# Weight products placed between the halves of the neighbour products, y high copied ahead of relu, and neighbour marks turned by DMA transposes

## The reference

```
d2  = sq[:, :, None] + sq[:, None, :] - 2.0 * einsum('bdn,bdm->bnm', xyz, xyz)   # xyz: 1601 x 512 per batch
_, idx = top_k(-d2, 8)
for i in range(4):                       # done twice, with the same weights
    p = lrelu(points, 0.01)
    g = the eight neighbours' columns of p
    points = (w_center[i] @ p + (w_neighbor[i] @ g).sum(over neighbours)) / 9 + points
```

## Time and profile before

| | |
|---|---|
| median of 3 runs | 337.64 us (336.52 to 339.07) |
| profiled execution, its own time | 334.24 us |
| its span, first to last instruction | 332.5 us |
| around the span | 1.74 us |
| TensorE matmul busy | 320.8 us (97%) |
| VectorE / ScalarE / GpSimd busy | 258.5 / 174.0 / 95.0 us |
| Gram phase, to the first step's first matmul | 107.17 us |
| granted TensorE clock | 1.00 throughout |

### The profile page before, as it was taken

The page is one execution under the profiler, slowest core; times in us unless marked ns, Lnnn a source line. Parts: engine busy times, 40 slices in busy tenths (PEclk is TensorE's granted clock), DMA queues, the critical chain, the costliest instruction groups (busy, mean ns, idle before and its releaser), DMA issues.

```text
span 332.5 us, 5114 instructions
## 1 busy us (share of the span) xinstructions
PE 320.8 (97%) x2024; PEld 290.9 (88%) x2024; DVE 258.5 (78%) x333; ACT 174.0 (52%) x255; POOL 95.0 (29%) x85
## 2 busy tenths in 40 slices
PE   4999999999999899999899999999999999999995
PEld 4999999999899788888788889888888888889884
DVE  3994799799699676888867796887869867796773
ACT  4584397485564726454836644626455264644510
POOL 2011111111133214333644441426335063441400
PEclk9999999999999999999999999999999999999999
DMA  7979859969700000000000000000000000000023
GB/s 236 353 209 264 223 146 239 279 150 251 188 0 1 2 0 2 0 0 2 1 2 0 1 3 0 0 2 0 2 0 0 2 0 2 0 0 2 38 92 126
DMA packets 8608, 23.41 MB, mean 70 GB/s; under 512 B 772, under 2 KB 2052, under 8 KB 8584
## 3 DMA queue, kind: packets, MB, share of 16 engines
q1 hardware_dynamic: 7288, 18.36, 16.3%
q0 software_dynamic: 1296, 4.72, 8.3%
HBM read 20.98 MB, written 2.10 MB: 69 GB/s over the span
## 4 chain that ended last, share of the span: by engine, by line
PE 41%; DVE 8%; ACT 2%; issue 1%; DVEq 0%
PE wide L423 24%; PE wide L412 6%; PE wide L401 5%; PE wide L399 5%; DVE y_rest L722 2%; DVE y_lo L726 2%; DVE r_mixed L662 2%; DVE state L734 2%; ACT y_hi L570 2%; ACT relu L562 1%; PE wide L385 0%; ACT r_high L565 0%; DVEq L709 0%; DVEq L725 0%
## 5 line engine op out<-in xcount | busy, mean ns | idle before, releaser
L279 POOL TENSOR_TENSOR r_low<-relu,r_high 128x512 fp32r<-128x512 f32 x64 | 84.8, 1339 | 140.4 <-ACT r_high L565 140.4
L423 PE MATMUL wide<-adj,y_hi 128*128 128x512 f32 (+1 forms) x260 | 102.3, 394 | 0.8 <-DVE state L734 0.8
L423 PE MATMUL wide<-adj,y_lo 128*128 128x512 f32 (+1 forms) x260 | 101.7, 393 | 0.0
L722 DVE TENSOR_TENSOR y_rest<-wide,y_hi 128x1024 f32<-128x1024 f32 x32 | 39.2, 1224 | 45.4 <-ACT y_hi L570 45.4
L562 ACT ACTIVATE relu<-state 128x512 f32<-128x512 f32 x64 | 40.2, 628 | 46.5 <-DVE state L734 33.7
L399 PE MATMUL wide<-w_high,r_high 128*128 128x256 f32 x256 | 62.2, 281 | 0.9 <-DVE y_rest L722 0.9
L401 PE MATMUL wide<-w_low,r_low 128*128 128x256 f32 x256 | 61.9, 280 | 0.0
L570 ACT CAST y_hi<-wide 128x1024 fp32r<-128x1024 f32 x32 | 32.3, 1008 | 54.8 <-PE wide L401 54.8
L423 PEld LDWEIGHTS wide<-adj,y_hi 128*128 128x128 f32 x260 | 48.9, 188 | 11.7 <-DVE state L734 1.2
L423 PEld LDWEIGHTS wide<-adj,y_lo 128*128 128x128 f32 x260 | 49.0, 188 | 10.5 <-issue 0.2
L399 PEld LDWEIGHTS wide<-w_high,r_high 128*128 128x128 f32 x256 | 48.3, 189 | 2.3 <-issue 1.1
(11 more groups left out here) (57 smaller groups left out, 290.6 us busy)
## 6 DMA issues: line engine op xcount, KB each, us to landing
raw<-in_ctx_dram SPq DMA_DIRECT2D x23, 512.0 KB, 5.4
g_low<-in_ctx_dram POOLq DMA_DIRECT2D x9, 512.0 KB, 6.2
state<-in_x_dram SPq DMA_DIRECT2D x4, 512.0 KB, 7.1
out_dram<-state SPq DMA_DIRECT2D x3, 512.0 KB, 2.8
w_raw<-in_fside_BxSxS_dram SPq DMA_DIRECT2D x1, 1024.0 KB, 11.2
rest_raw<-in_ctx_dram SPq DMA_DIRECT2D x4, 130.0 KB
raw<-in_ctx_dram SPq DMA_DIRECT2D x2, 256.0 KB, 3.3
out_dram<-state SPq DMA_DIRECT2D x1, 256.0 KB, 2.0
```

What stands on the lines that cost most here:

```text
L279: nc.gpsimd.tensor_tensor(r_low[:, n % 3, h, :], relu[:, h, :], r_high[:, n % 3, h, :].bitcast(fp32), ALU.subtract).then_inc(r_low_ready, 1)
L423: mm = nc.tensor.matmul(bank[to][:, cols], part[:, s % 2, q, h * P:(h + 1) * P], adj[:, b, q, cols], start=(q == 0 and part is y_hi), stop ...
L722: nc.vector.tensor_tensor(y_rest[:, :, :], wide[MAIN][:, :].rearrange("p (q o) -> p q o", q=NB), y_hi[:, s % 2, :, :].bitcast(fp32), ALU.s ...
```

## The change

1. **TensorE order in a step.** `y_step` is cut into `y_main` and `y_mixed`. A step is now: main products of s, first half of the neighbour products of s-1, mixed products of s, second half of the neighbour products of s-1.
2. **ScalarE order in a step.** `y_high(s)` comes first, then `relu_parts(s + 1)`.
3. **VectorE order in a step.** y_rest, update of half 0, y_lo, update of half 1, `relu_mixed(s + 1)`. For batch 3, distances and neighbours come one step earlier.
4. **Turning the marks.** The TensorE transposes are gone. SyncE issues four DMA transposes per batch, SBUF to SBUF, of 128x512 bf16 each (128 KB), into a new tile `turned`. For batch 0 they stand in SyncE's queue ahead of the point loads of batch 3, for batches 1 to 3 behind all loads. `copy_adj` reads `turned` instead of PSUM and waits for all four transposes of its batch; in the Gram phase it now comes after `copy_low`, and for batch 2 it comes in step 1, also after `copy_low`.
5. **Waits.** `square_row` waits for `copy_low` of the batch before instead of `copy_adj`. The last step uses banks 6, 7 and 0 and waits only for the updates of step 29.

```diff
--- before.py
+++ after.py
@@ -101,6 +101,7 @@
         half_sq = sb("half_sq", [P, NB], fp32)
         top8 = sb("top8", [P, NB, K], fp32)
         nbr = sb("nbr", [P, NB * (N + P)], bf16)
+        turned = sb("turned", [P, NB, N], bf16)
         adj = sb("adj", [P, B, NB, N], fp32r)
         ident = sb("ident", [P, P], fp32)
         eyes = sb("eyes", [P, NB, P], bf16)
@@ -119,11 +120,11 @@
         wide = [es.enter_context(nc.psum_tensor(f"wide{i}", [P, 2 * N], fp32)) for i in range(4)]
         bank = [wide[i // 2][:, (i % 2) * N:(i % 2 + 1) * N] for i in range(8)]
         MAIN_BANK, MIXED_BANK = 0, 3
-        SQ_BANK, LOW_BANKS, TR_BANKS = 6, (7, 6), (6, 7)
+        SQ_BANK, LOW_BANKS = 6, (7, 6)
         MAIN, MIXED, FIRST_WIDE, SECOND_WIDE = 0, 1, 2, 3
 
         ALL = slice(0, N)
-        LAST_OUT = ((0, ALL, 4), (1, slice(0, N // 2), 5), (1, slice(N // 2, N), 0))
+        LAST_OUT = ((0, ALL, 6), (1, slice(0, N // 2), 7), (1, slice(N // 2, N), 0))
 
 
 
@@ -144,6 +145,8 @@
 
         def out_at(s):
             return FIRST_WIDE if s < ENTER or s % 2 == 0 else SECOND_WIDE
+
+        assert out_at(LAST_STEP) == SECOND_WIDE
 
         def by_dma(b, k):
             return b > 0 and k in BY_DMA
@@ -235,6 +238,14 @@
                 else:
                     sp.dma_start(rest_raw[0:REST, :], ctx_4096[b, KT * P:POINT_DIM, :]).then_inc(unit_in[k], 16)
 
+            def turn_neighbours(b):
+
+                sp.wait_ge(self_added, b + 1)
+                if b > 0:
+                    sp.wait_ge(adj_ready, 2 * b)
+                for i in range(NB):
+                    sp.dma_start_transpose(turned[:, :, i * P:(i + 1) * P], nbr_rows[:, i, :]).then_inc(nbr_turned, 16)
+
             def load_state(b):
                 sp.dma_start(state[:, b, :, :], x[b, :, :].rearrange("(h p) n -> p h n", p=P)).then_inc(x_in[b], 16)
 
@@ -245,10 +256,14 @@
                 load_unit(0, k)
             sp.dma_start(w_raw[:, :, :, :], fside.rearrange("l (h p) i -> p l h i", p=P)).then_inc(w_in, 16)
             for b in range(1, B):
+                if b == B - 1:
+                    turn_neighbours(0)
                 for k in range(UNITS):
                     load_unit(b, k)
                 load_state(b - 1)
             load_state(B - 1)
+            for b in range(1, B):
+                turn_neighbours(b)
             for s in sorted(FINAL):
                 b = STEPS[s][1]
                 if s < LAST_STEP:
@@ -355,7 +370,7 @@
             def square_row(b):
 
                 if b > 0:
-                    pe.wait_ge(adj_ready, 2 * b)
+                    pe.wait_ge(low_copied, b * NB)
                 else:
                     pe.wait_ge(w_high_ready, BLOCKS)
                     pe.wait_ge(w_rest_ready, BLOCKS)
@@ -375,18 +390,7 @@
                                              dist[:, j, 3 * P:4 * P], ident[:, :])
                 mm.then_inc(low_turned, 1)
 
-            def turn_neighbours(b):
-
-                pe.wait_ge(self_added, b + 1)
-                for g in range(2):
-                    pair = bank[TR_BANKS[g]][:, :].bitcast(bf16)
-                    for jj in range(2):
-                        for i in range(NB):
-                            mm = nc.tensor.transpose(pair[:, jj * N + i * P:jj * N + (i + 1) * P],
-                                                     nbr_rows[:, i, (2 * g + jj) * P:(2 * g + jj + 1) * P], eyes[:, 0, :])
-                    mm.then_inc(nbr_turned, 1)
-
-            def y_step(s, w):
+            def y_main(s, w):
 
                 if s == 0:
                     pe.wait_ge(main_copied, B * NB)
@@ -401,6 +405,9 @@
                         mm = nc.tensor.matmul(dst, r_low[:, s % 3, h, q * P:(q + 1) * P], w_low[:, w, h, :],
                                               start=False, stop=(h == CH - 1))
                 mm.then_inc(main_done, 1)
+
+            def y_mixed(s, w):
+
                 if s == 0:
                     pe.wait_ge(gram_ready, (B - 1) * NB + 3)
                 pe.wait_ge(r_mixed_ready, s + 1)
@@ -415,7 +422,7 @@
 
             def out_step(s, b, pieces):
 
-                for n, (h, cols, to) in enumerate(pieces):
+                for n, (h, cols, to) in pieces:
                     for q in range(NB):
                         if n == 0 and q == 0:
                             pe.wait_ge(y_lo_ready, s + 1)
@@ -426,12 +433,10 @@
                     mm.then_inc(out_done, 1)
 
             def out_pieces(s):
-                return LAST_OUT if s == LAST_STEP else tuple((h, ALL, 2 * out_at(s) + h) for h in range(CH))
+                return enumerate(LAST_OUT if s == LAST_STEP else ((h, ALL, 2 * out_at(s) + h) for h in range(CH)))
 
             for b in range(B):
                 main_products(b, 0)
-                if b >= 2:
-                    turn_neighbours(b - 2)
                 main_products(b, 1)
                 mixed_products(b, 0)
                 if b > 0:
@@ -461,11 +466,12 @@
             pe.wait_ge(w_ready, BLOCKS)
             pe.wait_ge(w_mixed_ready, BLOCKS)
             for s, (l, b) in enumerate(STEPS):
-                y_step(s, l % BLOCKS)
+                y_main(s, l % BLOCKS)
                 if s == 0:
-                    turn_neighbours(B - 2)
+                    y_mixed(s, l % BLOCKS)
+                if s == 0:
+                    square_row(B - 1)
                 if s == 1:
-                    square_row(B - 1)
                     pe.wait_ge(gram_ready, B * NB)
                 if s > 0:
                     if s - 1 <= STEPS.index((0, B - 2)):
@@ -476,13 +482,14 @@
                         pe.wait_ge(state_ready, CH * (s - 1))
                     elif s - 1 > 0:
                         pe.wait_ge(state_ready, CH * (s - 1 if out_at(s - 1) == out_at(s - 2) else s - 2))
-                    out_step(s - 1, STEPS[s - 1][1], out_pieces(s - 1))
-                if s == 2:
+                    first_half, second_half = out_pieces(s - 1)
+                    out_step(s - 1, STEPS[s - 1][1], [first_half])
+                    y_mixed(s, l % BLOCKS)
+                    out_step(s - 1, STEPS[s - 1][1], [second_half])
+                if s == 1:
                     turn_distances(B - 1)
-                if s == ENTER - 1:
-                    turn_neighbours(B - 1)
-            pe.wait_ge(state_ready, CH * LAST_STEP)
-            out_step(LAST_STEP, STEPS[LAST_STEP][1], LAST_OUT)
+            pe.wait_ge(state_ready, CH * (LAST_STEP - 1))
+            out_step(LAST_STEP, STEPS[LAST_STEP][1], out_pieces(LAST_STEP))
 
         @block.scalar
         def _(act):
@@ -528,16 +535,14 @@
 
                 act.wait_ge(marked_ready, b * NB + 2 * g + 2)
                 if b > 0:
-                    act.wait_ge(nbr_turned, 2 * b)
+                    act.wait_ge(nbr_turned, 16 * NB * b)
                 nc.scalar.activation(nbr_rows[:, 2 * g:2 * g + 2, :], marked[:, 2 * g:2 * g + 2, :], ACT.Prelu,
                                      scale=1.0 / TAKEN, alpha=0.0).then_inc(nbr_ready, 1)
 
             def copy_adj(b):
+                act.wait_ge(nbr_turned, 16 * NB * (b + 1))
                 for g in range(2):
-                    act.wait_ge(nbr_turned, 2 * b + g + 1)
-                    nc.scalar.copy(adj[:, b, 2 * g:2 * g + 2, :],
-                                   bank[TR_BANKS[g]][:, :].bitcast(bf16).rearrange("p (j n) -> p j n", j=2))\
-                        .then_inc(adj_ready, 1)
+                    nc.scalar.copy(adj[:, b, 2 * g:2 * g + 2, :], turned[:, 2 * g:2 * g + 2, :]).then_inc(adj_ready, 1)
 
             def weights_high(l):
 
@@ -585,9 +590,9 @@
             for b in range(1, B):
                 points_parts(b, 5)
                 points_parts(b, 6)
+                copy_low(b - 1)
                 if b >= 2:
                     copy_adj(b - 2)
-                copy_low(b - 1)
                 if b == 1:
                     for l in range(BLOCKS):
                         act.wait_ge(w_rest_ready, l + 1)
@@ -608,19 +613,19 @@
                     copy_main(b)
                     neighbour_marks(b - 1, 1)
             for s in range(B * LAYERS):
+                y_high(s)
                 if s + 1 >= B - 1 and s + 1 <= LAST_STEP:
                     relu_parts(s + 1)
-                y_high(s)
                 if s == 0:
+                    relu_parts(2)
+                if s == 1:
+                    copy_low(B - 1)
                     copy_adj(B - 2)
-                    relu_parts(2)
-                if s == 2:
-                    copy_low(B - 1)
-                if s == 5:
+                if s == 4:
                     neighbour_marks(B - 1, 0)
-                if s == 7:
+                if s == 6:
                     neighbour_marks(B - 1, 1)
-                if s == ENTER:
+                if s == 8:
                     copy_adj(B - 1)
 
         @block.vector
@@ -714,13 +719,16 @@
                 dve.wait_ge(nbr_ready, 2 * b + 2)
```

(23 more changed lines are left out.)

## The result

| | before | changed |
|---|---|---|
| median of 20 runs each | 337.2 us (335.76 to 339.46) | 339.11 us (338.08 to 340.04) |
| ratio | | 1.0049, 95% interval 1.0031 to 1.0066 |
| profiled execution, its own time | 334.24 us | 339.23 us |
| its span | 332.5 us | 337.3 us |
| start of step 0 / step 3 / step 31 | 107.17 / 127.16 / 318.35 us | 106.15 / 125.97 / 324.08 us |

The change makes the kernel slower by 1.9 us; 4.4 us was forecast. The two profiled executions differ by 5.0 us. The mechanism of the stall was as forecast; most of the miss lies between one execution of the kernel before and its usual ones.

What follows compares the result with a forecast made beforehand. TensorE was taken as the bound, 6.60 us of work in a 6.83 us step. Terms -2.5 + 8.0 - 0.2 - 0.9 = +4.4 on the profiled 334.24 gave 338.6, carried to the median as 342.0 us; range 336 to 348.

Steps and rivals of the forecast that it cites:

- Part 3: Steps 3 to 31: TensorE waits for r_low in every step, period 7.11 us, +8.0 us over 28 periods.
- Part 2: DMA transposes: 7 to 9 us a batch, hidden before ScalarE's copy_adj; nothing paid up to some 11 us.
- Part 4: Steps 0 to 2: last main product of step 3 at 128.83 us against 129.00, -0.2 us.
- Part 5: The end: last neighbour products follow the last main product at 4.82 us, before at 5.74, -0.9 us.
- Part 1: Gram phase: transposes leave TensorE (1.9 us) and a wait for the adj copy goes (about 0.6 us), -2.5 us.
- the sum: Whole kernel: -2.5 + 8.0 - 0.2 - 0.9 = +4.4 us against the profiled 334.24 us, so 338.6 us.
- I carry the difference over: Whole kernel: profiled execution lies 1% under the median 337.64 us; the difference is added, taking 338.6 to 342.0 us.

Runs made afterwards that it cites:

- experiment 2: The changed kernel with ScalarE's order undone, relu_parts(s+1) ahead of y_high(s) again: 327.69 us, ratio to before 0.9748.
- experiment 3: The kernel before with one edit, y_high(s) ahead of relu_parts(s+1) on ScalarE: 343.46 us, ratio to before 1.0208.
- experiment 7: The changed kernel with relu_parts(s+1) cut in two, half 0 ahead of y_high(s), half 1 behind it: 326.24 us, ratio to before 0.9708.
- experiment 4: The kernel before with the DMA transposes and their waits alone, step order kept: 332.63 us, ratio to before 0.9888.
- experiment 5: The kernel before with copy_adj(b-2) moved ahead of points_parts(b, 5) and (b, 6) in the Gram phase: 334.07 us, ratio to before 0.9933.
- the two later profiles: The kernel before, unchanged, profiled a second and a third time: 337.32 us, ratio 1.0019, and 336.59 us, ratio 0.9992.
- the third profile: The kernel before, unchanged, profiled once more: 336.59 us, ratio 0.9992, profiled span 336.0 us.

## Why the prediction was wrong

It said slower, and it is slower, for the reason given; the size was wrong, +4.4 us against +1.9.

- *Part 3, the r_low chain: right.* Links of 0.32, 0.91, 1.38 and 2.55 us against 0.31, 0.91, 1.38 and 2.55; the release took 0.05 and not 0.10. Period 7.07 to 7.08 against 7.11; 28 periods cost 324.08 - 125.97 - 191.19 = +6.9 us against +8.0, so 1.1 too much came of 0.04 us in each. Experiments 2, 3 and 7 show the cause from three sides.
- *Part 2, the transposes: right.* Under 10.7 us a batch, no copy waited, and experiment 4 found no price on the side of the DMAs; what it found on the side of TensorE's clock is not in this kernel.
- *Parts 4 and 5: right.* Steps 0 to 2 take 0.17 us less (forecast 0.2); from the start of step 31 to the end it is 13.2 us against 14.15, 0.9 less (forecast 0.9).
- *Part 1, in the profile:* before its last products the Gram phase was 1.96 + 0.64 = 2.6 us ahead, forecast 2.5. That VectorE would be next there I didn't see; 0.94 us were given back. -1.0 (with 0.64 of late start) - 0.2 + 6.9 - 0.9 = +4.8 us, the difference of the spans. That this is so near the +4.4 of the sum is partly luck: the 1.1 us too much in part 3 and the 0.94 us given back, which the sum had at nothing, nearly cancel.
- *Where it failed.* The step was in part 1, "with the slow mixed products before it about 0.6 us", and in the sum, "I carry the difference over". The price of the removed wait was read from one execution, which was also the shortest of the kernel before: 334.24 us, under all of its 20 ordinary ones. Measured by itself (experiment 5) the wait costs 2.2 us in ordinary executions, 1.6 more than I took (1.5 and 1.8 us by the two later profiles); the first row of squares of that execution came at 36.96, against 37.45 to 37.70 in eight other profiles and 39.52 in one, so it started some 0.6 us early, without regard to the kernel. Taken off the 5.0 us between the profiled executions they leave 2.8; measured is 1.9 (1.0 to 2.2 by the interval). The rest, about 0.9 us (1.4 with the price from the profiles), I can't place: a start as late as in the third profile is part of ordinary executions, but how often it comes in either kernel wasn't measured. The stretch it belongs to can be estimated: from step 0 to the end the three profiles of before took 225.2 to 225.3 us, so a run at the median, with a span of about 335.4, reaches step 0 at about 110.2 and not at 107.17, while the changed kernel's profile lies at its own median.

The sign that I had and read the wrong way: the profiled execution lay 1% under the median and below the lowest of three runs. I treated that as a constant to add to both kernels. Part of it was a wait of the kernel before that the change removes.

## What to carry to other kernels

When the order of two jobs on one engine is exchanged, follow the chain from the event that the first one waits for through all that now stands behind it: 0.4 us too long, in every step, outweighed all that the change removed. Cutting the longer job in two, one half on each side, took the whole stall away. And a wait behind a transfer has no single price: where the profiled execution is faster than the ordinary runs, look for waits of that kind in the profile and price them by more than one execution, or by moving the waiting job alone. Last, look at what fills the place of work that is taken away: in experiment 4 the transposes had cost nothing where they stood, and the idle time that they left went with a lower clock and 1.5 us.

## What the runs showed of the hardware

- Four 128x512 bf16 DMA transposes within SBUF held SyncE's queue 7.36 us beside loads, 1.8 us each, and landed 5.6 us after issue; alone they landed in 2.5 us.
- GpSimd's r_low and VectorE's r_mixed, both on SBUF alone, hold each other up, and here the one that had started first went through: an r_mixed that started 0.19 us after a 1.30 us r_low took 2.19 us and ended 1.08 us after it, where it takes 1.22 alone (experiment 2); an r_low that started beside an r_mixed took 2.27. y_lo, which also reads PSUM, kept its 1.23 us beside r_low.
- After 1.88 us without a matmul TensorE's granted clock fell from 1.00 to 0.50 for some 3.5 us, starting 1 us after it had resumed; after 0.92 and 0.96 us in the same place it stayed at 1.00 (experiment 4).
- Three profiles of one kernel differed by up to 3.5 us, all of it before the first step; from there to the start of the last they repeated to 0.1 us.
